# Attention heads on 64 array rows each, three PSUM banks for the scores, outputs stored untransposed and divided by their sums in the next stage

## The reference

```python
scale = 1.0 / jnp.sqrt(jnp.float32(D)).astype(x.dtype)          # D = 16
scores = jnp.einsum('bqhd,bkhd->bhqk', q, k) * scale            # 1024 x 1024 per head
probs = jax.nn.softmax(scores, axis=-1)
out = jnp.einsum('bhqk,bkhd->bqhd', probs, v).reshape(B, S, H)
return out @ wo.T
...
h = x + _attention(_rmsnorm(x, ln1_w), wq, wk, wv, wo)
h = h + _moe(_rmsnorm(h, ln2_w), gate_w, w1, w2, w3)
```

## Time and profile before

| | us |
|---|---|
| median of 3 runs | 3612.48 (3611.93 to 3614.39) |
| the profiled execution | 3616.42 |
| its span, first to last instruction | 3614.8 |
| PE busy in the span | 3226.5 (89%) |
| DVE busy | 2386.9 (66%) |
| ACT busy | 1894.9 (52%) |
| POOL busy | 584.8 (16%) |

### The profile page before, as it was taken

One profiled execution on the slowest core, in us unless ns is written; L12 is line 12 of the kernel. 1 busy time (PEld: TensorE's weight loads), 2 busy tenths in 40 slices (PEclk: granted clock), 3 DMA queues, 4 the chain that ended last, 5 costly groups with the idle time before them and its releaser, 6 DMA issues. The chain is left out here.

```text
span 3614.8 us, 64942 instructions
## 1 busy us (share of the span) xinstructions
PE 3226.5 (89%) x19056; PEld 2116.2 (59%) x19057; DVE 2386.9 (66%) x4072; ACT 1894.9 (52%) x3374; POOL 584.8 (16%) x846
## 2 busy tenths in 40 slices
PE   5888888849999999999999999997956999999980
PEld 4766666634545455454554545544845888888870
DVE  5666666648888878878878878862567444444436
ACT  3555555513676666666666666664523333333320
POOL 1222222210000000000000000000123444444430
PEclk7899989968999999999999999998878999999995
DMA  1333333321111111111111111114932111111119
GB/s 33 105 104 104 104 104 104 109 99 52 41 54 45 49 51 43 54 41 53 46 48 53 41 54 43 51 31 141 289 105 81 47 51 51 49 49 51 49 46 367
DMA packets 195841, 279.74 MB, mean 77 GB/s; under 512 B 26792, under 2 KB 129472, under 8 KB 195792
## 3 DMA queue, kind: packets, MB, share of 16 engines
q1 hardware_dynamic: 154320, 209.90, 17.9%
q0 software_dynamic: 16128, 44.06, 3.9%
q10 hardware_dynamic: 25344, 25.17, 2.2%
HBM read 158.37 MB, written 118.49 MB: 77 GB/s over the span
## 5 line engine op out<-in xcount | busy, mean ns | idle before, releaser
L779 DVE TENSOR_REDUCE b_mxq<-b_p_m 128x1 f32<-128x1024 f32 x1024 | 1205.5, 1219 | 312.7 <-PE b_p_m L833 304.6
L737 ACT ACTIVATE b_probs<-b_p_e 128x512 f32<-128x512 f32 x2048 | 1112.0, 595 | 509.6 <-PE b_p_e L887 504.8
L887 PE MATMUL b_p_e<-b_qst,b_kst 128*128 128x512 f32 x2048 | 799.7, 436 | 5.9 <-ACT b_probs L737 5.9
L887 PEld LDWEIGHTS b_p_e<-b_qst,b_kst 128*128 128x128 f32 x2048 | 343.5, 187 | 599.6 <-ACT b_probs L737 577.2
L833 PE MATMUL b_p_m<-b_kst,b_qst 128*128 128x512 f32 x2048 | 645.3, 402 | 29.9 <-DMA b_vst<-v_d 24.5
L862 PE MATMUL b_p_o<-b_probs,b_vst 128*32 128x512 f32 x4104 | 546.5, 605 | 0.9 <-ACT b_probs L737 0.9
L833 PEld LDWEIGHTS b_p_m<-b_kst,b_qst 128*128 128x128 f32 x2048 | 388.0, 191 | 116.6 <-issue 24.9
L1443 ACT ACTIVATE d_act<-d_p_up 128x512 f32<-128x512 f32 x136 | 81.3, 597 | 487.3 <-PE d_p_up L1505 487.3
L753 POOL DMA_DIRECT2D o_d<-b_o_s x64 | 34.8, 544 | 1637.9 <-DVE b_o_s L805 1637.9
L1520 PE MATMUL d_p_y<-w2T,d_hT 128*128 x1096 | 258.7, 379 | 0.8 <-ACT d_hT L1437 0.8
L1505 PE MATMUL d_p_up<-up_hi,d_xh 128*128 x544 | 250.7, 461 | 1.5 <-DVE d_xl L1462 1.5
(11 more groups left out here) (259 smaller groups left out, 4160.5 us busy)
## 6 DMA issues: line engine op xcount, KB each, us to landing
b_qst<-qk_d SPq DMA_DIRECT2D x384, 64.0 KB
b_kst<-qk_d SPq DMA_DIRECT2D x384, 64.0 KB
x1y_d<-a_x1y SPq DMA_DIRECT2D x32, 512.0 KB, 3.9
qk_d<-a_hi SPq DMA_DIRECT2D x32, 512.0 KB, 2.8
qk_d<-a_lo SPq DMA_DIRECT2D x32, 512.0 KB, 3.7
v_d<-a_v_s SPq DMA_DIRECT2D x16, 1024.0 KB, 6.9
b_vst<-v_d SPq DMA_DIRECT2D x64, 256.0 KB
c_xy<-x1y_d SPq DMA_DIRECT2D x16, 1024.0 KB
```

Source lines behind the costliest of these rows:

```text
L737: nc.scalar.activation(probs[e // 2 % 4][:, (e % 2) * 512:(e % 2 + 1) * 512], p_e[e % 2][:], ACT.Exp, scale=SCALE).then_inc(s["e_done"], 1)
L779: V_.reduce_max(mxq[half][:, j:j + 1], p_m[j % 2][:], AX.X).then_inc(s["m_red"], 1)
L887: mm(p_e[a][:], kst[r][h][:, kt * P:(kt + 1) * P], qst[r][:, a * 512:(a + 1) * 512], start=True, stop=True).then_inc(s["e_ps"], 1)
```

## The change

In attention:

- One key tile for both heads; `rows(h)` picks rows 0 to 63 or 64 to 127 of both operands, so each score product runs on 64 array rows. Product 4*kt+e of the maxima stands right behind score product e of step kt, and it belongs to the other head (`column`), so that it uses the other 64 rows.
- Three banks `p_e` in place of two. A bank's turn also goes once per pair to the transpose of the maxima.
- The output transposes, the reciprocal and the multiplication by it leave. ACT, and no longer DVE, copies `p_o` into one of two tiles `oT`, and POOL stores that: 32 rows per head and half, of which row 16 holds the sums.
- POOL splits the maxima into high and low parts ahead of the transpose.

In the projection:

- SP loads the sums of a block (`den_in`), DVE takes their reciprocals (`rec`), ACT stores these to DRAM (`rd_d`), and SP loads them back with each row repeated 16 times (`rd`, 512 KB).
- POOL multiplies `oin` by `rd` into `oT` (1024 columns). ACT's reordering and copy and PE's eight transposes leave.

```diff
+    EB = 3
+    SLOTS = 4 * KT + 1
-    kst = [[sb(f"kst{r}_{h}", [P, N], f32r) for h in range(2)] for r in range(RING)]
+    kst = [sb(f"kst{r}", [P, N], f32r) for r in range(RING)]
+    NEG_AT = 10
+    def slot(e):
+        return e if e <= NEG_AT else e + 1
+    def column(j):
+        return 1 - j % 2, j // 2
...
@@ scalar, attention
+        def evacuate(n, half):
+            act.wait_ge(s["pv_done"], n * KT + 2)
+            act.wait_ge(s["o_free"], n + 1)
+            nc.scalar.copy(oT[half][:], p_o[:]).then_inc(s["oT_done"], 1)
...
+                if e == 2:
+                    evacuate(pair, r % 2)
...
@@ tensor, attention
-            h, qt = j // 8, j % 8
+            h, qt = column(j)
             if kh == 0:
                 pe.wait_ge(s["m_red"], pair * 16 + (j + 1))
-            mm(p_m[j % 2][:, kh * 512:(kh + 1) * 512], qst[r][:, qt * P:(qt + 1) * P], kst[r][h][:, kh * 512:(kh + 1) * 512], start=True, stop=True).then_inc(s["m_ps"], 1)
+            mm(p_m[j % 2][:, kh * 512:(kh + 1) * 512], qst[r][rows(h), qt * P:(qt + 1) * P], kst[r][rows(h), kh * 512:(kh + 1) * 512], start=True, stop=True).then_inc(s["m_ps"], 1)
...
             for kt in range(KT):
-                scores(kt, 0)
-                if kt > 0 and more:
-                    max_half(pair + 2, r2, 4 * kt - 1)
-                scores(kt, 1)
...
-                    values(pair, r, kt - 1)
-                scores(kt, 2)
-                scores(kt, 3)
-                if more:
-                    for m in range(4 * kt, 4 * kt + 3 + (kt == KT - 1)):
-                        max_half(pair + 2, r2, m)
...
+                for e in range(4):
+                    scores(kt, e)
+                    if more:
+                        max_half(pair + 2, r2, 4 * kt + e)
+                    if 4 * kt + e == NEG_AT and more1:
+                        pe.wait_ge(s["e_done"], pair * SLOTS + (NEG_AT + 2))
+                        max_transpose(pair + 1, (NEG_AT + 1) % EB)
+                    if e == 2:
+                        if kt == 1:
+                            pe.wait_ge(s["oT_done"], pair + 1)
+                        values(r, kt - 1, pair * SLOTS + ((slot(4 * kt - 1) if more1 else 4 * kt - 1) + 4))
...
@@ sync, projection
+        def load_inverses(half, b):
+            sp.wait_ge(s[f"rec_st{half}"], b * 16 + 16)
+            sp.sem_inc(s["sp_turn"], 1)
+            for k in range(2):
+                sp.dma_start(rd[half][:, k], rd_d[b, half, 8 * k:8 * k + 8].rearrange("g (o q) -> g o q", o=1).to_broadcast([8, 16, HT])).then_inc(s[f"rd{half}"], 16)
...
+        def body(n, half, b, b_next, before, after, after2):
+            if after2:
+                sp.wait_ge(s["recip_done"], n + 1)
+                sp.sem_inc(s["sp_turn"], 1)
+                load_sums(half, b + 1)
             if after:
                 if before:
-                    sp.wait_ge(s["orow_done"], n)
-                load_output(n + 1, 1 - half, b_next)
+                    sp.wait_ge(s["oT_done"], n)
+                    sp.sem_inc(s["sp_turn"], 1)
+                load_output(1 - half, b_next)
+                load_inverses(1 - half, b_next)
             sp.wait_ge(s["in_free"], n + 1)
             sp.dma_start(xy[half][:], x1y_v[n]).then_inc(s[f"in{half}"], 16)
...
@@ gpsimd, projection, at the end of body(n)
+            if after:
+                normalised(n + 1, 1 - half, b_next, before)
@@ scalar, projection, at the end of body(n), behind the squares
+            if after2:
+                store_inverses(n + 2, half, b + 1)
@@ vector, projection, body(n)
             if before:
                 choose(n - 1)
+            if after2:
+                inverses(n + 2, half, b + 1)
             dve.wait_ge(s["r_done"], n1)
```

More of the change, by code:

```diff
@@ L708, in _ @@
             for h in range(2):
-                sp.dma_start(kst[r][h][R * h + 48:R * h + 50, :].bitcast(f32), ones[:]).then_inc(s[f"rows{r}"], 16)
+                sp.dma_start(kst[r][R * h + 48:R * h + 50, :].bitcast(f32), ones[:]).then_inc(s[f"rows{r}"], 16)
             if r < 3:
                 load(r, r)
-        maxima(0, 0, 0)
+        maxima(0, 0, EB)
         def body(pair, i, r, more1, more, more3):
-            if more1:
-                maxima(pair + 1, (r + 1) % 2, (r + 1) % RING)
             if more3:
@@ L720, in body @@
                 load(pair + 3, (r + 3) % RING)
+            if more1:
+                maxima((r + 1) % 2, (r + 1) % RING, pair * SLOTS + (NEG_AT + 5))
         pairs(sp, body)
@@ L869, in _ @@
                 pe.wait_ge(s[f"rows{r}"], 32)
-            for j in range(16):
-                max_scores(pair, pair, j)
+            for half in range(32):
+                max_half(pair, pair, half)
             if pair == 0:
-                max_transpose(0, 0)
+                max_transpose(0, EB - 1)
         for g in range(4):
@@ L1026, in store, with body @@
             act.dma_start(xg_v[n], xg[half][:]).then_inc(s[f"st{half}"], 16)
-        gather_features(0, 0, 0)
-        transposed(0, 0)
-        def body(n, half, b, b_next, before, after):
+        for half in (0, 1):
+            store_inverses(half, half, 0)
+        act.wait_ge(s["w_in"], 48)
+        def body(n, half, b, b_next, before, after, after2):
             n1 = n + 1
-            if after:
-                gather_features(n + 1, 1 - half, b_next)
             if before:
@@ L1037, in body @@
                 store(n - 1, 1 - half)
-            if after:
-                transposed(n + 1, 1 - half)
             act.wait_ge(s["h_done"], n1)
@@ L1056, in _, with inverses @@
             dve.sem_inc(s[n], c)
+        def inverses(n, half, b):
+            if not isinstance(b, int) or b > 0:
+                dve.wait_ge(s[f"rec_st{half}"], b * 16)
+            dve.wait_ge(s[f"den{half}"], b * 16 + 16)
+            V_.reciprocal(rec[half][:], den_in[half][:]).then_inc(s["recip_done"], 1)
+        for half in (0, 1):
+            inverses(half, half, 0)
         dve.wait_ge(s["wT_ps"], 1)
@@ L1140, in router, with body @@
             i.then_inc(s["lg_ps"], 1)
-        output_transposes(0, 0)
-        def body(n, half, b, b_next, before, after):
+        def body(n, half, b, b_next, before, after, after2):
             n1 = n + 1
@@ L1154, in body @@
                 router_transposes(n - 1, 1 - half)
-            if after:
-                output_transposes(n + 1, 1 - half)
             if before:
```

213 lines of the change are left out of this document (91 added, 122 removed).

## The result

The changed kernel takes 3817.11 us, the median of 4 runs (3802.21 to 3823.11); the kernel before takes 3613.43 beside it. The ratio is 1.0557 (95% interval 1.0527 to 1.0588), so it is slower by 204 us, where the forecast said 96 (3709). The profiled execution takes 3817.9; by it attention grew by 62 us (from its start to the last store of a pair, 1738.5 against 1676.4), the projection from its start to its last `h` by 129 (277.2 against 148.5), and the rest by about 10: 2 ahead of attention, and 8.6 from the last `h` to the end (990.9 against 982.3). What moves it is open.

What follows compares the result with a forecast made beforehand. Attention was taken as bound by a ring through ACT, 3.10 us a step; projection blocks took 8.85 us. The profiled 3616.4 + 8 (attention) + 88 (projection) = 3712, or 3709 against the runs' median; range 3630 to 3800.

Steps and rivals of the forecast that it cites:

- The ring that goes: Attention: the chain through ACT's exponentials falls to 2.59 us a step, 0.51 less than before the change.
- The ring that comes: Attention: the chain through the second maxima buffer, around the values, sets a step of 3.17 us, against 3.10 before.
- upper bound of 3.28: Attention: the longest step in the forecast's range, with 0.16 us between the two products of a pair.
- Row overlap: Attention: score and maxima products on separate 64 array rows overlap, starting 0.05 us apart.
- The first ring: Projection: the serial chain from landed residuals through the reciprocals' store and reload to the next residuals, 13.4 us a block.
- My bound: Projection: the block's upper bound of 17 us, from a 3.0 us store plus both rings touching.
- The 14.7 of the forecast: Projection: the length of the first ring if a transfer's fixed part is 2.0 us, in place of 13.4.
- The second ring: Projection: the chain through squares, root, POOL's product, PE's line 1151, transposes and scaling: 12.5 us, or 15.0 at the lower clock.
- The surviving prefetch: Projection rival: residuals still land before they are needed, costing only some 15 us: 3632 us in all, chance 6%.
- The first rival: Attention: the maxima don't decide, the 2.59 us ring sets every pair, 280 us less: 3421 us in all, chance 5%.

Runs made afterwards that it cites:

- e1: The changed kernel with attention's values products moved from behind the third score and maxima product of a step to behind the fourth: 3574.2 us.
- e2: The changed kernel with the projection's residuals load issued at the head of SP's part, ahead of the wait for the stored reciprocals: 3776.5 us.
- e10: The changed kernel with the residuals' load issued ahead of the load that spreads the reciprocals, behind the same wait: 3774.0 us.
- e3: The changed kernel with the maxima products on the same 64 array rows as the score products beside them: 3908.1 us.
- e11: e6 with each row of the reciprocals stored twice and read as 16 rows, as in e7: 3539.3 us.
- e7: The changed kernel with each row of the reciprocals stored twice, so that their load reads 16 rows eight times: 3813.9 us.
- e6: The changed kernel with the edits of e5 and e1 together: 3521.4 us.
- e14: e6 with the two large stores of the block before issued behind the small store of the reciprocals on ACT: 3512.0 us.
- e5: e2 with GpSimd's product of block n+1 ahead of its root of block n: 3762.4 us.

## Why the forecast was wrong in size

**The sign and both mechanisms were right.** The maxima decide the step, through the buffer whose halves stand on either side of the values (e1 takes only that away and gains 243); and the residuals behind the reciprocals decide the block (e2, e10).

**The ring that goes.** 2.59 forecast, 2.61 measured in the last pairs.

**The ring that comes.** The term that failed in attention is the end of the sum, 0.05 to the second maxima product and 0.43 from there to the reduction: 0.48 forecast, 0.00 + 0.56 measured. The overlap was better than I took it, the duration worse. I read 0.43 from the second of three products in the earlier trace rows, which starts hot; the earlier trace rows had the cold one beside it, two products in 0.73 of which the second starts 0.33 late. The other terms were 1.27 + 0.43 + 0.99 against 1.28 + 0.43 + 0.99. The step is 3.27 and not 3.17, a pair 26.35 and not 25.56, and 62 pairs make 49 of the 54 us by which attention was missed. The forecast's upper bound of 3.28 held.

**Row overlap.** Starts less than 0.1 apart were right (0.00 to 0.01). The Trainium skill, "TensorEngine Tiling (Array Packing)", Overview, gives up to 2x for a small dimension of at most 64. In the trace the two products start together and are done after 0.49 to 0.50, where the two on the same rows in e3 need 0.34 + 0.40; the overlap was worth 0.19 us of this ring.

**Projection.** The first ring to the store's landing: 4.85 + 2.0 forecast (h and base, choose, reciprocal; store), 2667.62 - 2660.75 = 6.87 measured. The term that failed here is the load of the reciprocals and the residuals, 1.57 MB in 6.3 us: with the 0.25 for semaphores 6.55, where the block shown took 9.5 and the mean of twelve is 10.3. It counted one fixed part and bytes at full speed. In its place stand the landing of the residuals themselves (6.4 for 1.05 MB with nothing ahead in e10) and what is issued ahead of it (3.1, of which SP's issuing, put at nothing in the sum, is 1.6). Rows of the profile before pointed there and I passed over them, the median landings of a 1 MB store of the first stage, of a 1 MB load of the experts and of a 512 KB load of this stage (view of DMA issues: KB each, median us):
```profile
v_d<-a_v_s SPq DMA_DIRECT2D x16, 1024.0 KB, 6.9
...
e_ys<-ys_d SPq DMA_DIRECT2D x16, 1024.0 KB, 9.1
...
c_oin<-o_d SPq DMA_DIRECT2D x16, 512.0 KB, 5.1
```
My bound used only the 512 KB store of 3.0. The Trainium skill's 2.0 us fixed ("DMA: Bandwidth & Descriptors", Anatomy of one DMA, a section on DMAs issued from GpSimd, while these come from SP and ACT) would by my estimate have added 0.65 to the chain, of the 3.0 that were missing. The 14.7 of the forecast added it twice, though its store stood at 2.0 already. The small store's median landing of 1.5 does not bear the figure out.

**The second ring** was forecast at 12.5 or 15.0 and is 14.3 in e2; I took 15.0 for the block because of it. With 16.8 the serial ring is the longer, so the value was right within 2 us for the wrong reason. The lower clock came as forecast (0.69), with line 1157 at 6.4 and not 5.4. The stage was missed by 41 us: (16.76 - 15.0) x 15 = 26; a 15th interval, which I had not counted, 6; and a first `h` 25.8 behind the stage's start, 10 later than before (15.75) and not 2, another 8. The 10 us outside the two stages (first paragraph) had no term in the sum at all.

**A sum among the rivals.** The surviving prefetch was put at 3632; by its own terms, 3709 - 88 + 15, it is 3636. Nothing rests on the difference.

**The first rival** (maxima don't decide, 3421, 5%) is what e1 builds: it gives 3574 with the projection as it is, so attention gains 243 and not 288, at 2.69 a step and 22.4 a pair (the mean of 63 intervals of its stores), where 20.9 was taken.

## What to carry to other kernels

When a wait is taken out of a pipeline, follow each buffer that has two writers around it: a buffer whose halves are filled on either side of a long group of instructions pays for the whole group in its ring, however idle its reader looks. A load that was prefetched is prefetched only as long as nothing that waits for this block's results is issued ahead of it on the same queue; the order on the queue is a dependency. For a load on the critical path use the landing time of a transfer of the same size, not the engines' bandwidth, and add the time in which its queue issues what stands ahead of it. Before a difference between two runs is put down to the edit, compare them stage by stage: the 18 us of e11 lie in a stage that its edit doesn't touch.

## What was not expected of the hardware

A product behind the values takes 0.50 us where the next takes 0.39, and both of a pair on separate rows take it, since they start together. A load of 8 rows spread over 128 partitions keeps the DMA engines at a share of 0.51, one of 16 rows at 0.85, and the chain behind it gets only 0.5 us shorter (e7). The last two pairs of attention run at a granted clock of 1.0 in e1, e6 and e14 and of 0.5 in e11, with the same instructions. GpSimd's product of 1024 columns (2.34 us) beside DVE's four multiplications by the root makes these last 3.22 us and not 1.14:
```profile
2665.76 2.34 POOL L1002 TENSOR_TENSOR c_oT<-c_oin,c_rd 128x1024 f32<-128x1024 f32 x1
2665.82 3.22 DVE L1110 TENSOR_SCALAR c_xg<-c_h,c_r_s 128x256 f32<-128x256 f32 x4 [0.15 <-POOL c_r_s L1012]
```
In e5, where the product stands elsewhere, the four take 1.14 again; `base`, which the product can then meet, takes 1.23 in the median block and up to 2.74.
